# One TensorE loop rotated: the branch of the recurrent loop moves from in front of step 0's first gates to behind them

## The reference, cut to what matters

```python
# first layer, a gated unit
z = sigmoid(xzt + h @ U_z + vz)
r = sigmoid(xrt + h @ U_r + vr)
hh = tanh(xht + r * h @ U + vh)
h = (1.0 - z) * h + z * hh            # x1 = x + h
# second layer, over x1
gate = sigmoid(h1 @ Wh.T + x1_t @ Wz.T + b)
h1 = tanh(h1 * leak + gate * x1_t)    # x2 = x1 + h1
```

## Time and profile before

| what | value |
|---|---|
| time, median of 3 runs | 989.01 us (987.12 to 990.15) |
| the profiled execution's own time | 990.85 us |
| its span, first to last instruction | 989.0 us |
| TensorE busy | 943.0 us (95%) |
| VectorE busy | 802.5 us (81%) |
| ScalarE busy | 647.3 us (65%) |
| mean granted TensorE clock | 0.976 |

### The profile page before, as it was taken

The page is one execution under the profiler, slowest core; times in us unless marked ns, Lnnn a source line. Parts: engine busy times, 40 slices in busy tenths (PEclk is TensorE's granted clock), DMA queues, the critical chain, the costliest instruction groups (busy, mean ns, idle before and its releaser), DMA issues.

```text
span 989.0 us, 112546 instructions
## 1 busy us (share of the span) xinstructions
PE 943.0 (95%) x50966; PEld 766.4 (77%) x50966; DVE 802.5 (81%) x2372; ACT 647.3 (65%) x2862; POOL 221.2 (22%) x430
## 2 busy tenths in 40 slices
PE   6699999999999999999999999969999999999996
PEld 5699999999999999999999998335555555555554
DVE  2378778878788778777878787799999999999992
ACT  2478777777777777777777776336455556555552
POOL 0011111111111111111111111324434334434340
PEclk7699999999999999999999999979999999999998
DMA  6113312310010100100101001100011000001001
GB/s 218 41 55 112 110 50 95 111 35 27 24 37 24 37 24 27 34 27 24 37 24 37 24 27 33 28 1 25 24 37 34 24 24 24 24 31 41 24 24 43
DMA packets 38294, 42.01 MB, mean 42 GB/s; under 512 B 5120, under 2 KB 31232, under 8 KB 37120
## 3 DMA queue, kind: packets, MB, share of 16 engines
q1 hardware_dynamic: 36832, 40.55, 13.2%
q10 hardware_dynamic: 1440, 1.18, 0.4%
HBM read 32.80 MB, written 8.91 MB: 42 GB/s over the span
## 4 chain that ended last, share of the span: by engine, by line
PE 57%; DVE 29%; issue 7%; ACT 4%; DMA 1%; ACTq 1%; POOL 0%; DVEq 0%; POOLq 0%
PE bank L788 30%; PE bank L734 22%; DVE arena L667 10%; DVE early L686 4%; DVE early L677 4%; ACT cand_kept L391 2%; DVE early L690 2%; DVE early L684 2%; DVE early L671 2%; DVE early L665 2%; DVE none_h L604 2%; PE bank L906 2%; PE bank L923 1%; DMA bias<-in_bias 1%; PE bank L877 1%
## 5 line engine op out<-in xcount | busy, mean ns | idle before, releaser
L734 PE MATMUL bank<-x_ahead,early 128*32 128x64 f32 x12376 | 345.7, 224 | 5.9 <-ACT bank L358 3.2
L734 PEld LDWEIGHTS bank<-x_ahead,early 128*32 128x32 f32 x12376 | 239.7, 111 | 3.3 <-issue 3.3
L788 PE MATMUL bank<-none_h,early 128*32 128x32 f32 x16384 | 203.1, 199 | 8.8 <-issue 4.9
L280 POOL TENSOR_TENSOR x<-x_f,h_gx 128x64 f32 x256 | 87.6, 342 | 529.4 <-PE bank L788 528.3
L788 PEld LDWEIGHTS bank<-none_h,early 128*32 128x32 f32 x16384 | 180.6, 110 | 27.4 <-DVE none_h L604 13.5
L906 PE MATMUL bank<-x,wl 128*128 (+1 forms) x384 | 182.3, 614 | 0.9 <-DVE rank_rows L646 0.9
L788 PE MATMUL bank<-rh_f,early 128*32 128x32 f32 x8192 | 151.0, 199 | 5.0 <-DVE rh_f L592 2.2
L906 PEld LDWEIGHTS bank<-x,wl 128*128 128x128 f32 x384 | 69.2, 192 | 89.0 <-issue 89.0
L788 PEld LDWEIGHTS bank<-rh_f,early 128*32 128x32 f32 x8192 | 122.1, 112 | 7.0 <-DVE rh_f L592 5.0
L604 DVE TENSOR_TENSOR_SCAN none_h<-zero_z,cand_kept 128x64 f32<-128x64 f32 x512 | 121.6, 279 | 5.3 <-ACT cand_kept L391 3.9
L402 ACT ACTIVATE h_gx<-h_pre 128x64 f32<-128x64 f32 x256 | 68.7, 268 | 81.0 <-DVE h_pre L630 81.0
(11 more groups left out here) (95 smaller groups left out, 1294.4 us busy)
## 6 DMA issues: line engine op xcount, KB each, us to landing
x_in<-in_x SPq DMA_DIRECT2D x34, 256.0 KB, 2.7
x_ahead<-in_x SPq DMA_DIRECT2D x130, 64.0 KB, 1.8
arena<-in_w SPq DMA_DIRECT2D x8, 1024.0 KB, 5.6
out<-y SPq DMA_DIRECT2D x32, 256.0 KB, 2.5
rank_rows<-in_bias_rows SPq DMA_DIRECT2D x1, 1024.0 KB, 5.0
arena<-scratch SPq DMA_DIRECT2D x64, 16.0 KB
early<-in_cx SPq DMA_DIRECT2D x1, 768.0 KB, 4.5
early<-in_wx SPq DMA_DIRECT2D x1, 768.0 KB, 6.3
```

The costliest lines, as they stand in the source:

```text
L280: pool.tensor_tensor(x2[:, :, :, s], x1_f[:, u % LOOP], h1_gx[:, u % 2, :, :, 0], ALU.add).then_inc(x2_done, 1)
L734: mm = pe.matmul(out[32 * j:32 * j + 32], weights(k, j, m), moving(k), start=False, stop=False, tile_position=(0, 32 * j), skip_group_chec ...
L788: mm = pe.matmul(out[32 * j:32 * j + 32], weights(k, j, m), moving(k), start=False, stop=k == 1, tile_position=(0, 32 * j), skip_group_che ...
```

## The change

The first gates of step 0, with their four late products ahead, are taken out of the head of the turn. They are issued once before the loop and again at the end of each turn, for the turn that follows. The work and its order stay what they were; only the place of the branch in it changes. At the end of the last turn the gates are computed once more, for a step 256 that does not exist; nobody uses them.

```diff
+            def gates_of_turn():
+                first_gates(0, late_keep=lambda: ahead_first(0, 1, 1, (1,)))
+
             def turn():
-                first_gates(0, late_keep=lambda: ahead_first(0, 1, 1, (1,)))
                 second_gate(0)
                 first_cand(0, hole=lambda: loaded(1, 0, 0, (0,)))
...
                 ahead_first(0, 1, 0)
                 ahead_first(0, 1, 1, (0,))
+                gates_of_turn()
...
+            gates_of_turn()
             with nc.Fori(0, T // LOOP, engines=bass.OrderedEngineSet([pe.engine]), hint_back_edge=True):
                 turn()
```

## The result

| what | before | after |
|---|---|---|
| median of 4 runs each, us | 988.07 (986.96 to 990.15) | 1002.36 (1000.96 to 1005.29) |
| ratio, 95% interval | | 1.0146 (1.0114 to 1.0178) |
| the profiled execution, us | 990.85 | 1001.25 |
| its span, us | 989.0 | 999.4 |

The change makes the kernel slower by 14.3 us in the medians, 1.5%. The forecast was 996.3 us with a range of 991.5 to 1001.0: the sign was right, the size outside the range. (The median before is 0.94 us lower than the 989.01 that the forecast started from, since a fourth run is in it.

What follows compares the result with a forecast made beforehand. It took TensorE's loop steps, scan to scan, as the bound, with the branch delaying step 0's gates. Profiled 990.85 + 7.2 for later second-layer loads + 0.1 behind the loop = 998.15, less 1.84: 996.3 us, range 991.5 to 1001.

Steps and rivals of the forecast that it cites:

- The branch leaves its place before the gates: At step 0's gates: removing the branch there gives back 0.08 us in 48 turns, at most 3.8 us.
- The gap in the new place: Between the last late load and the second layer's first load: 0.39 us, bounds 0.33 and 0.55.
- the 0.22: The most, in us, that TensorE's sequencer could get ahead of the array over 40 wide loads before the branch.
- The bound of 0.55 for a lead lost whole: Gap at the new branch place if the sequencer's whole lead is missing: 0.31 us more a turn, 14.9 us.
- The two chains: From the second layer's late load, via candidate (2.44 us) or second gate and gate*x1 (2.46): 0.15 us a turn, 7.2 us.
- The common turns: The 15 turns where ScalarE's and VectorE's loops turn too: nothing gained or added, upper bound 2.4 us.
- The rest, 0.1 us: Behind the last turn: 36 extra products lie in a wait, delaying the second layer's load by 0.1 us, at most 0.27.
- The hidden branch: Rival: the branch fits into the 0.12 us of room before the second layer's load; 3.8 us gained, 985.2 us; chance 0.06.
- the half-hidden one: Rival: gap about 0.33 us or a little less, gate*x1 not holding the scan; 986 to 992 us; chance 0.09.
- the sign for a lead lost whole: In the profile after: a step 0 longer than 2.6 us would show the sequencer's lead lost whole.
- Lost code: Rival: the loop's code no longer stays on the chip, a 1.75 us stall each turn; 110 us, 1099 us; chance 0.03.

Runs made afterwards that it cites:

- c4: The changed kernel with the second layer's 16 products of step 0 also moved ahead of the branch; ratio to the kernel before 1.0169.
- c1: The changed kernel run once more with nothing altered; 1000.28 us against 987.04 for the kernel before, ratio 1.0139.
- d4: The kernel before with eight steps instead of four in each turn of TensorE's loop; 1934.27 us, then 1940.04 on another chip.
- e1: The kernel before with 30 idle products long before the loop, which only move all later code; ratio 1.0008.
- e2: The changed kernel with 30 idle products long before the loop, which only move all later code; 997.15 us, ratio to the kernel before 1.0094.
- d2: The changed kernel without the prefetch hint at the head of TensorE's loop; ratio to the kernel before 1.0065.
- c5: The kernel before with the branch moved up by 12 products, behind the first 8 of step 3's 20 wide ones; one run, 995.31 us against 988.90.
- c3: The kernel before with the branch moved in front of all 20 wide products of step 3; ratio 1.0103.
- d1: The kernel before without the prefetch hint at the head of TensorE's loop; ratio 1.0022.
- c2: The kernel before with only the 36 extra products for step 256 added behind the loop, the branch unmoved; ratio 1.0026.

## Why the forecast had the sign and missed the size

*The branch leaves its place before the gates.* Right. The waits are gone, and the gates come 0.34 us after the scan.

*The gap in the new place.* The first step that failed: "I take 0.39: of the 0.22 I believe half ... and of that half I let half be lost." The gap measured 0.45 us in the mean (0.46 in the turn shown). The sequencer's lead in the old place was 0.14 us; the 0.11 that the prediction believed came near it by luck. But more than half of it was lost: 0.04 is left, so almost three quarters went, and the turn itself took 0.02 us longer. The bound of 0.55 for a lead lost whole was too wide, since it stood on 0.22; with all of 0.14 lost the gap would be 0.47. Halving twice was a guess put in the place of the one question that decided, and the start times of the branch's own records in the trace of the kernel before would have given the 0.14 and the 0.46 of the turn.

*The two chains.* Right in form. With 0.45 in place of 0.39 the prediction's own chain reads 1.01 + 0.45 + 0.57 + 0.25 + 0.24 = 2.52 us; the mean is 2.54. 48 turns x (2.52 - 2.31) = 10.1 us in place of 7.2, and the loop's count gives 10.3. That gate*x1 holds the scan can't be told from the candidate's chain, which ends as late: its second part starts 0.19 us behind the first (430.22 to 430.41) instead of 0.15, and in c4, where gate*x1 is early, the step is as long.

*The common turns.* Right within 0.02 us a turn (2.56 against 2.54 in the mean).

*The rest, 0.1 us.* The second failed step, and the larger one: 4.4 us were missed here, 3.1 in the loop. The extra products themselves are nearly hidden, as the prediction had it: the second layer's first load comes 1.29 us after the last state (622.56 against 621.27) instead of 1.13. What it didn't see is that 36 more products shift the code behind the loop, and that the first packet of instructions behind the exit starts only 1.2 us after the last branch. That cost 4.5 us in the profiled execution and 2.8 in c1. The kernel before has no such stall, but its own first packet behind the loop starts after the exit too, at 613.70 us, and the earlier trace rows showed the kind of stall in the first turns. Either miss alone would have left the time inside the range (996.3 + 3.1 or 996.3 + 4.4); it took both to leave it.

*The rivals.* The hidden branch is refuted: a gap of 0.45 is far over the 0.12 of room. So is the half-hidden one, which had 0.33. The prediction had no row for the branch by itself; the trace has one, 0.216 us before and 0.223 after, and that alone is longer than the room. Nor was the sign for a lead lost whole, a step longer than 2.6, of use: it stood on the 0.22. Lost code did not happen in this kernel, and 12 packets were the right evidence. But its price was set too low: d4 lost 950 us, not 110, since there the body that didn't fit was fetched whole and not by one block.

**What stays open.** Why a stall at the exit comes or not. The place of the code decides in e1 and e2, but d2 has no stall either, with one instruction less in the loop and no hint, and c5's exit is the longest of all. The instruction queue adds a hint, no more: by about the end of the first turn e2 and d2 had fetched eight packets, the changed kernel and c1 seven, c3 and c5 six. But the kernel before has no stall with seven. What the missing hint does eight loads behind the branch in d1, and not in d2, isn't known either.

## What to carry to other kernels

A loop's branch on TensorE cost here what the sequencer did not have in hand when it came to it: 0.46 us less the lead. Of the places tried, the best was behind the longest run of wide products, although the gates right behind it were urgent. The worst were the two with four wide products or none in front and the second layer's or the candidate's products behind. Read the price as the gap between two load starts, and the lead from the starts of the branch's own records, since the list of waits names whatever semaphore is last there. When products are added or moved, look at the first blocks behind the loop's exit too, and compare with a version whose code is only shifted.

## What the runs showed of the hardware

- A turn of the loop takes TensorE's sequencer 0.46 to 0.48 us with the prefetch hint (0.36 to 0.37 without), wherever it stands. What shows is that less the sequencer's lead: a gap of 0.33 us between two loads behind 40 wide loads (lead 0.14), and of 0.45 behind 64 narrow and 8 wide (lead 0.04). The Trainium skill, "Advanced Engine Details and Errata", Control Flow Timing, has some 108 ns for a compare-and-branch; this trace does not agree: its record takes 216 ns before and 223 after.
- The prefetch hint for the branch is not free: without it the gap is 0.23 instead of 0.33, and 0.33 instead of 0.45. Without it the changed kernel's loop is 5.8 us shorter and the kernel before slower (1.0022). (The changed kernel's ratio of 1.0065 without the hint, against 1.0146, also has 4.4 us of exit in it.)
- A loop of 384 products went through 63 branches back without a fetch; one of 768 was fetched whole in every turn, and the kernel took 1.97 times as long.
- A fetch behind a loop's exit stalled TensorE for 1.9 to 4.4 us (c2 and c4), and 30 idle products far ahead of the loop bring the stall or take it away. In the stalled kernels TensorE goes on 2.3 to 2.7 us after the packet's start.
